# Second attention: results of odd head groups packed into the unused rows of even groups

## The reference

```python
q = jax.nn.elu(q) + 1.0
k = jax.nn.elu(k) + 1.0
kv = jnp.einsum('blhd,blhe->blhde', k, v)
kv_cumsum = jnp.cumsum(kv, axis=1)
k_cumsum = jnp.cumsum(k, axis=1)
out = jnp.einsum('blhd,blhde->blhe', q, kv_cumsum)
normalizer = jnp.clip(jnp.einsum('blhd,blhd->blh', q, k_cumsum), 1e-06, None)
out = out / normalizer[..., None]
out = out.reshape(b, l, HIDDEN)
return out @ Wo.T
```

## Time and profile before

| | |
|---|---|
| median of 3 runs | 2052.06 us |
| lowest, highest | 2045.66, 2052.25 us |
| span of the profiled execution | 2049.7 us |
| TensorE busy | 1891.4 us (92%) |
| VectorE busy | 1243.8 us (61%) |
| GpSimd busy | 1256.3 us (61%) |
| ScalarE busy | 935.0 us (46%) |
| mean granted clock of TensorE | 0.972 |

### The profile page before, as it was taken

How to read it: one execution, slowest core, us unless ns; L and a number is a source line. 1 busy time by engine, 2 the same in 40 slices (tenths; PEclk the granted TensorE clock), 3 DMA queues, 4 the chain that set the end, 5 groups by cost and what they waited for, 6 DMA issues and landing times. The chain is left out here.

```text
span 2049.7 us, 35437 instructions
## 1 busy us (share of the span) xinstructions
PE 1891.4 (92%) x12820; PEld 1311.8 (64%) x12820; DVE 1243.8 (61%) x1863; ACT 935.0 (46%) x1613; POOL 1256.3 (61%) x818
## 2 busy tenths in 40 slices
PE   6998899999999999999999987888985999998998
PEld 5887444544545445454544546666764899998998
DVE  5775566666566675656666545776762666656343
ACT  5885334334243443434334324333320557676554
POOL 3553688778687886878878654456454463435433
PEclk8999799999999999999999999999997999999999
DMA  4243232132231322313232123132224532423222
GB/s 140 103 133 120 77 83 54 40 93 78 73 80 34 93 63 67 79 32 94 62 87 59 32 52 111 43 95 68 61 79 135 169 83 42 131 44 82 42 43 42
DMA packets 83521, 158.78 MB, mean 77 GB/s; under 512 B 15036, under 2 KB 65244, under 8 KB 77652
## 3 DMA queue, kind: packets, MB, share of 16 engines
q1 hardware_dynamic: 64512, 119.85, 21.6%
q0 software_dynamic: 14592, 18.40, 5.5%
q10 hardware_dynamic: 4288, 18.81, 2.5%
HBM read 80.32 MB, written 44.71 MB: 61 GB/s over the span
## 5 line engine op out<-in xcount | busy, mean ns | idle before, releaser
L1197 ACT ACTIVATE a_pr<-a_pT 128x1024 f32<-128x1024 f32 x256 | 262.1, 1024 | 425.2 <-PE a_pT L953 425.2
L1232 POOL TENSOR_TENSOR a_total<-a_total,a_pr 128x1024 f32<-128x1024 f32 x128 | 318.8, 2491 | 149.7 <-ACT a_pr L1197 149.4
L1062 DVE TENSOR_REDUCE a_row_max<-a_pG 128x2 f32<-128x1024 f32 x256 | 309.1, 1220 | 145.4 <-PE a_pG L927 145.1
L966 PE MATMUL a_pA<-a_pr,a_v 128*64 128x512 f32 x1024 | 277.0, 619 | 0.1
L2257 DVE TENSOR_TENSOR c_h_lo<-c_h,c_h_hi 128x256 fp32r<-128x256 f32 x288 | 152.2, 534 | 180.3 <-ACT c_h_hi L2212 171.2
L2212 ACT ACTIVATE c_h<-c_pU,c_b_c 128x256 f32<-128x256 f32 x288 | 141.3, 491 | 169.1 <-PE c_pU L105 167.7
L1232 POOL TENSOR_TENSOR a_total<-a_pr 128x1024 f32<-128x1024 f32 x64 | 151.7, 2371 | 52.1 <-ACT a_pr L1197 51.8
L1213 POOL TENSOR_TENSOR a_by_cos<-a_by_cos,a_swapped 128x1024 f32<-128x1024 f32 x64 | 154.5, 2415 | 31.3 <-DMA a_swapped<-a_by_sin 31.3
L1220 POOL TENSOR_TENSOR a_qk_lo<-a_by_cos,a_qk_hi 128x1024 fp32r<-128x1024 f32 x64 | 158.7, 2480 | 2.3 <-ACT a_qk_hi L1166 2.3
L1056 DVE TENSOR_TENSOR a_by_sin<-a_pG,first_sin 128x1024 f32<-128x1024 f32 x64 | 78.4, 1224 | 134.4 <-PE a_pG L105 130.5
L2310 POOL DMA_INDIRECT out_x<-c_y,c_ids x72 | 118.9, 1651 | 40.9 <-DVE c_y L2273 27.5
(11 more groups left out here) (297 smaller groups left out, 4980.0 us busy)
## 6 DMA issues: line engine op xcount, KB each, us to landing
a_swapped<-a_by_sin SPq DMA_DIRECT2D x256, 128.0 KB, 2.3
a_inv_by_head<-mid_inverses SPq DMA_DIRECT2D x30, 512.0 KB, 6.0
c_raw<-in_weights ACTq DMA_DIRECT2D x5, 2048.0 KB, 12.2
c_x_t<-mid_rows SPq DMA_DIRECT2D x36, 272.0 KB, 2.9
mid_latents<-f_c_parts SPq DMA_DIRECT2D x8, 1024.0 KB, 4.3
first_latents<-mid_latents SPq DMA_DIRECT2D x8, 1024.0 KB, 7.5
f_x_t<-in_x SPq DMA_DIRECT2D x8, 512.0 KB, 3.7
mid_part<-f_out SPq DMA_DIRECT2D x16, 256.0 KB, 2.3
```

The source lines that it names most:

```text
L966: last = nc.tensor.matmul(pA[64 * h:64 * h + 64, :], v[:, t, p, h, :], pr[:, n % RP, h, :], start=(t == 0), stop=(t == NT - 1))
L1062: nc.vector.reduce_max(row_max[:, u % 2, :, t], pair[:], AX.X).then_inc(read, 1)
L1197: nc.scalar.activation(pr[:, n % RP, :, :], pT[:], ACT.Exp, scale=SCALE).then_inc(exp_done, 1)
L1232: nc.gpsimd.tensor_tensor(total[:, u % 2, :, :], before, pr[:, n % RP, :, :], ALU.add).then_inc(summed, 1)
```

## The change

Before a batch is normalised, four transfers (one for each j) copy the 16 result rows of each odd group (1 and 3) into the 16 rows below those of the even group ahead of it (0 and 2), over the denominators, which have by then been read out. An even group then has 128 rows of results, in the order of the reference's heads. `normalise` takes the two even groups alone and waits for these copies (`odd_in`) too; `inv_rows` has two groups of 128 rows, filled by 8 transfers (j, i) in place of 4; `project_out` takes two products, and `wo` is laid out as it comes.

```diff
--- before.py
+++ after.py
@@ -1280,7 +1280,7 @@
         blocks = sb("blocks", [P, 8, CL])
         before = sb("before", [P, NE, NE])
         bg_row = sb("bg_row", [P, NE])
-        wo = sb("wo", [P, 4, D])
+        wo = sb("wo", [P, 2, D])
         names = {"q": (wq_t, KC * D), "k": (wk_t, KC * D), "v": (wvg_t, KC * VG)}
         w_hi = {n: sb(f"w{n}_hi", [P, f], F32R) for n, (_, f) in names.items()}
         w_lo = {n: sb(f"w{n}_lo", [P, f], F32R) for n, (_, f) in names.items()}
@@ -1305,7 +1305,7 @@
         part = sb("part", [P, NC1, 8, CL])
         o = sb("o", [P, 2, 4, S])
         den = sb("den", [P, 64])
-        inv_rows = sb("inv_rows", [P, 4, S])
+        inv_rows = sb("inv_rows", [P, 2, S])
         lg = sb("lg", [P, NT, NE])
         top = sb("top", [P, NT])
         tot = sb("tot", [P, NT])
@@ -1360,6 +1360,7 @@
         o_out = sem("o_out")
         den_out = sem("den_out")
         den_in = sem("den_in")
+        odd_in = sem("odd_in")
         inv_step = sem("inv_step")
         inv_out = sem("inv_out")
         inv_in = sem("inv_in")
@@ -1432,14 +1433,19 @@
                     sp.dma_start(dens[b % 2, :, :], o[16:P:32, b % 2, :, :].rearrange("j g q -> j (g q)")).then_inc(den_out, 16)
                     sp.wait_ge(den_out, 16 * (b + 1))
                     sp.dma_start(den[:], dens[b % 2, :, :].rearrange("j (r e) -> (j r) e", e=64)).then_inc(den_in, 16)
+                    for j in range(4):
+                        sp.dma_start(o[32 * j + 16:32 * j + 32, b % 2, 0:4:2, :],
+                                     o[32 * j:32 * j + 16, b % 2, 1:4:2, :]).then_inc(odd_in, 16)
                     sp.wait_ge(inv_step, 2 * b + 2)
                     sp.dma_start(invs[b % 2, :, :].rearrange("j (r e) -> (j r) e", e=64), den[:]).then_inc(inv_out, 16)
                     sp.wait_ge(inv_out, 16 * (b + 1))
                     if b >= 1:
                         sp.wait_ge(norm_done, NT * b)
                     for j in range(4):
-                        sp.dma_start(inv_rows[32 * j:32 * j + 16, :, :].rearrange("p g q -> p (g q)"),
-                                     invs[b % 2, j:j + 1, :].to_broadcast([16, 4 * S])).then_inc(inv_in, 16)
+                        for i in range(2):
+                            sp.dma_start(inv_rows[32 * j + 16 * i:32 * j + 16 * i + 16, :, :],
+                                         invs[b % 2, j:j + 1, :].rearrange("j (c i q) -> j c i q", i=2, q=S)[:, :, i, :]
+                                         .to_broadcast([16, 2, S])).then_inc(inv_in, 16)
 
                 def invert_half(h):
 
@@ -1449,13 +1455,18 @@
                     sp.dma_start(there.rearrange("(j g q) -> j g q", j=4, g=4), o[16:P:32, (B - 1) % 2, :, ts]).then_inc(den_out, 16)
                     sp.wait_ge(den_out, 16 * (B + h))
                     sp.dma_start(den[:, 0:32], there.rearrange("(p e) -> p e", e=32)).then_inc(den_in, 16)
+                    for j in range(4):
+                        sp.dma_start(o[32 * j + 16:32 * j + 32, (B - 1) % 2, 0:4:2, ts],
+                                     o[32 * j:32 * j + 16, (B - 1) % 2, 1:4:2, ts]).then_inc(odd_in, 16)
                     sp.wait_ge(inv_step, 2 * (B + h))
                     sp.dma_start(back.rearrange("(p e) -> p e", e=32), den[:, 0:32]).then_inc(inv_out, 16)
                     sp.wait_ge(inv_out, 16 * (B + h))
                     sp.wait_ge(norm_done, NT * (B - 1))
                     for j in range(4):
-                        sp.dma_start(inv_rows[32 * j:32 * j + 16, :, ts],
-                                     back.rearrange("(j g q) -> j g q", j=4, g=4)[j:j + 1, :, :].to_broadcast([16, 4, S // 2])).then_inc(inv_in, 16)
+                        for i in range(2):
+                            sp.dma_start(inv_rows[32 * j + 16 * i:32 * j + 16 * i + 16, :, ts],
+                                         back.rearrange("(j c i q) -> j c i q", j=4, c=2, i=2)[j:j + 1, :, i, :]
+                                         .to_broadcast([16, 2, S // 2])).then_inc(inv_in, 16)
 
                 def first_rows():
 
@@ -1597,9 +1608,9 @@
                 def project_out(b, t):
                     bank, done = begin("out", b, t)
                     pe.wait_ge(norm_done, NT * b + t + 1)
-                    for g in range(4):
-                        last = nc.tensor.matmul(bank[:, 0:D], o[:, b % 2, g, t * P:(t + 1) * P], wo[:, g, :],
-                                                start=(g == 0), stop=(g == 3))
+                    for c in range(2):
+                        last = nc.tensor.matmul(bank[:, 0:D], o[:, b % 2, 2 * c, t * P:(t + 1) * P], wo[:, c, :],
+                                                start=(c == 0), stop=(c == 1))
                     last.then_inc(done, 1)
 
                 def rank(b):
@@ -1721,9 +1732,11 @@
                     nc.vector.reciprocal(den[:, 0:wide], den[:, 0:wide]).then_inc(inv_step, 1)
 
                 def normalise(b, t):
-                    dve.wait_ge(inv_in, 64 * (b + 1) + 64 * (b == B - 1 and t >= 2))
+                    parts = b + 1 + (b == B - 1 and t >= 2)
+                    dve.wait_ge(odd_in, 64 * parts)
+                    dve.wait_ge(inv_in, 128 * parts)
                     ts = slice(t * P, (t + 1) * P)
-                    nc.vector.tensor_tensor(o[:, b % 2, :, ts], o[:, b % 2, :, ts], inv_rows[:, :, ts],
+                    nc.vector.tensor_tensor(o[:, b % 2, 0:4:2, ts], o[:, b % 2, 0:4:2, ts], inv_rows[:, :, ts],
                                             ALU.mult).then_inc(norm_done, 1)
 
                 def add_out(b, t):
@@ -2381,12 +2394,7 @@
 
 def by_group(m):
 
-    w = np.zeros((4, CL, 4, m.shape[1]), np.float32)
-    for g in range(4):
-        for j in range(4):
-            h = 8 * (g // 2) + 2 * j + g % 2
-            w[j, :DE, g, :] = m[DE * h:DE * h + DE]
-    return w.reshape(P, 4, m.shape[1])
+    return m.reshape(2, P, m.shape[1]).transpose(1, 0, 2)
 
 
 def lay_out(a):
```

## The result

| | before | changed | ratio (95% interval) |
|---|---|---|---|
| median, us | 2052.15 (20 runs) | 2040.66 (20 runs) | 0.9947 (0.9935 to 0.9958) |
| lowest, highest | 2045.66, 2057.48 | 2034.65, 2054.55 | |
| span of the profiled execution | 2049.7 | 2042.8 | |

The change takes 11.5 us away; 17.8 were forecast. The direction is right, and the time lies inside the range. The highest time of the changed kernel, 2054.55, is one execution at a mean granted clock of 0.92 (0.97 in the others, the next highest is 2045.80).

What follows compares the result with a forecast made beforehand. Bound taken: each round's loop from add_out through SP's five steps, normalising and products, then a chain at the stage's end. Savings of 14.8 + 1.7 + 1.3 = 17.8 us gave 2052.1 - 17.8 = 2034.3, range 2023 to 2048.

Steps and rivals of the forecast that it cites:

- the copies: Between denominators' return and inverses' way out: VectorE's inversion hides the issuing, inverses land undelayed; 0 taken, bounds 0 to +2.9.
- the end: End of the stage after the last round: shorter products and normalising against unhidden extra issues, 1.3 us saved in sum.
- Products: TensorE's output products of two blocks, once a round: eight passes for 16, 1.86 in place of 3.72, 1.86 us saved.
- Normalising: VectorE's first pair in a round: two operations of 256 columns at 0.76, 0.6 us taken as saved.
- Eight issues, x = 0: Spreading inverse rows by eight transfers for four: landing delay x taken as 0, between -0.8 and +1.7; issuing takes 3.42.
- One round: A round of the second attention: products 1.86 plus normalising 0.6 less the rows' delay, 2.46 us saved.
- Six rounds: The rounds of batches 1 to 6, each saving 2.46 us: 14.8 us together.
- The last round: The round without key features: between 0 and 3.5 us saved, depending on whether a later stall moves along; 1.7 taken.
- Late rows: Rival: the smaller pieces of inverse rows land as late after issue as large ones, x = +1.7; put at 2047, chance 0.15.
- Early rows: Rival: inverse rows land early enough that TensorE's whole 8.1 us wait in six rounds goes; 2029.8, chance 0.12.
- Inverses stuck behind the copies: Rival: copies ahead in the queue delay the inverses by 2.6 every round, each of six losing 1.8; near 2067, chance 0.07.
- The loop does not carry it: Rival: the round after the products has another clock, so only 3.6 and the ends are saved; 2045.5, chance 0.08.

Runs made afterwards that it cites:

- e1: The changed kernel without the four copies and the wait for them, odd heads' results left out: 2032.00 us, ratio 0.9901 to the kernel before.
- e6: The changed kernel with SP sending a batch's denominators and copies at the end of its own round, ahead of store and load: 2035.30 us, ratio 0.9924.
- e7: The kernel before with SP's first steps moved early, ahead of store and load, nothing packed: 2048.64 us, ratio 0.9989.
- e3: The kernel before with eight issues of inverse rows in place of four, same bytes: 2056.75 us, ratio 1.0020.
- e4: The changed kernel with the rounds' copies issued by ScalarE, not SP; the last batch's stay on SP: 2045.24 us, ratio 0.9966 to the kernel before.
- e10: e6 with VectorE's inversion of the last batch's first half moved ahead of batch 6's last add_outs: 2028.54 us, ratio 0.9876 to the kernel before.

## Why the prediction came out as it did

The mechanism was right: the loop from the add_outs over SP's five steps to the products does carry a round, and two products instead of four shorten it. Its size was off by 6 us, most of it by one term, the copies; the end is the second. A part of what was measured is luck: some 2.5 of the 11.7 us come from round 4, where before the inverses took 4.1 to land, which the forecast didn't count.

**The step that failed** is that of the four copies: "VectorE's inversion hides the issuing", and "I take 0, by the copy's row". Both halves fell. The issue took 2.51, not 1.71, and ended after VectorE. The landing was taken from large copies by themselves; what counted was a small transfer, the inverses, behind four copies, and it took 2.5 to 2.8 in place of 1.5. The copies' bounds were 0 to 2.9; from the denominators' return to the rows' first issue the rounds 2, 3 and 5 took 5.40, 5.75 and 5.53, against 3.96, 4.32 and 4.30 before: 1.2 to 1.4 each. In rounds 1 and 6 VectorE inverts late and the inverses land in 1.46 and 1.45: nothing lost. e1 prices the term, with what it brought behind the products (the wait for ScalarE in rounds 2 and 4, the low clock in round 3), at 7 to 9 us for the whole kernel. Two of the signs of being wrong showed: inverses over 2.5 on the way in three of four rounds, and rounds 2 and 3 about as long as before.

Term by term:
- *Products* 1.86 a round: measured 1.72 (2.00 against 3.72), except in round 3, in which the clock fell (0.15).
- *Normalising* 0.6: the pair takes the 0.76 that was read from the add_out, but 1.48, 1.22 and 0.72 were saved in rounds 2, 3 and 5, since the later pair no longer meets GpSimd's sum; a pair that comes earlier meets it (e6, e7).
- *Eight issues, x = 0*: right in the rounds (6.3 to 6.8 against 6.1 to 6.5 to VectorE's start; e3 leaves the rounds as they are), although issuing them took 4.45 to 4.87 and not 3.4.
- *One round* 2.46: 0.74 on average in rounds 2, 3 and 5. Saved were 1.14 from the normalising to the products and 1.32 from the products to the store; lost were 1.37 from the denominators' return to the rows' first issue, and 0.32 on the denominators' own way, which took 4.05 to 4.20 (3.52 to 4.14 before).
- *Six rounds* 14.8: measured 10.25, that is 1.65 + 0.46 - 0.05 + 3.31 + 1.81 + 3.07. In the 1.65 stand 2.65 that were lost ahead of the change's own transfers, and 2.5 of the 3.31 is the luck named above.
- *The last round* 1.7: measured 2.33, so its stall moved along for the most part.
- *The end*, forecast 1.3 shorter: 0.9 longer. Products of batch 6 gave 2.32 (2.7 forecast); the issues took 1.65 and 1.02 (1.8 and 1.7); the copies, forecast at nothing, took 0.8 (2.93 to the inverses against 2.34, and 1.68 against 1.43 to land); and of 2.1 for the last normalising and the last products 0.2 came, since eight passes at the lower clock take as long as sixteen at the upper.

**The rivals.** *Late rows* (2047) is as near to 2040.7 as the forecast, but not by its mechanism: rows aren't late, inverses are. *Early rows* fell: in rounds 2 to 5 VectorE starts 6.3 to 6.8 after the rows' first issue, 6.1 to 6.5 before. Only in round 1 it starts clearly sooner, 5.83 against 6.65, and there it had not waited for them. From the Trainium skill's rule on ports (page "SBUF — State Buffer", section "Door 1: The DMA port swizzle") the prediction drew that pieces on alternating partitions gain; the 6.3 to 6.8 do not support it. The Trainium skill's rule to merge small transfers (page "DMA: Bandwidth & Descriptors", section "Rules for kernel authors") agrees with e3's +0.20% as a whole, though the price came at the end of the stage and not in the rounds. *Inverses stuck behind the copies* had the mechanism and not the size: 1.0 in place of 2.6. *The loop does not carry it* has the nearest number (2045.5); e1 speaks against it, whose rounds are shorter by as much as the forecast put down to products and normalising, but the waits for ScalarE behind the products, 1.02 and 1.24, are of its kind.

Open: what holds the inverses for 4.1 in one round of the kernel before. Two of GpSimd's sends of rows lie in that stretch, but two lie beside the inverses of round 2 as well, which took 1.51; it wasn't tried apart. Open too: what holds ScalarE behind the products.

## What to carry to other kernels

A transfer put ahead of a small one that somebody waits for delays it: here the inverses by 1.0 to 1.1 us and, when the copies were on ScalarE's queue, the rows by about 1.5 (e4). Put it where nobody waits, here ahead of a store and 7 us before the inverses (e6), which then land in 1.47. Half the passes needn't be half the time where the engine has waited first (3.75 against 3.69 at the end): read the granted clock of the stretch that is to become shorter. And take the cost of an issue from the nearest kind of transfer, not from the next line.

## What the runs showed that was not expected

- Issuing a copy from one part of the on-chip memory to another took 0.63 us (2.51 for four), on SP's queue as on ScalarE's (2.54), with 64 KB as with 1 KB (2.52); a spread of rows from memory took 0.45 (3.59 for eight) at the end of the stage.
- Inverses behind four copies of 1 KB still landed 0.2 to 0.8 us later than without.
- Eight passes took 3.75 at granted clock 0.51 after 6.59 us of idle, and 1.97 at 1.00 after useless products and 0.68 of idle.
- Two VectorE operations of 256 columns took 0.76 alone, 1.07 beside GpSimd's scaling, 2.62 beside its scaling and its sum, and 4.99 beside its work on the next stage's weights (e10).
